# A four-layer graph kernel: largest score by transposes, earlier first attention steps, four accumulators in layer 0, eight buffers in layer 3

## What is computed

```python
# layer 0: normalised graph convolution
deg = sum(adj.T, axis=1); d = deg ** -0.5
x = x + (d[:, None] * adj.T * d[None, :]) @ (h @ W0) + b0
# layer 1: rows of adj, with 1/sqrt(count) added where adj > 0
inc = adj + (adj > 0) / max(sqrt(sum(adj > 0)), 1e-12)
x = x + (inc @ h) / sum(inc, axis=-1)
# layer 2: attention, 4 heads of 256, mean over the heads
ht = (h @ W2) per head; src = ht . a_src; dst = ht . a_dst
att = softmax(leaky_relu(src[:, None] + dst[None, :], 0.01) + adj)
x = x + mean over heads of att @ ht
# layer 3: binarised
x = x + relu(adj @ (max(sign(h), 0) @ sign(W3).T))
```

## Time and profile before

| | |
|---|---|
| median of 3 runs | 771.5 us (770.08 to 772.02) |
| profiled execution, its own time | 770.67 us |
| its span, first to last instruction | 768.8 us |
| mean granted clock of TensorE | 0.991 |
| PE busy | 729.3 us, 95% |
| DVE busy | 667.2 us, 87% |
| ACT busy | 458.7 us, 60% |
| POOL busy | 57.1 us, 7% |

### The profile page before, as it was taken

How to read it: one execution, slowest core, us unless ns; L and a number is a source line. 1 busy time by engine, 2 the same in 40 slices (tenths; PEclk the granted TensorE clock), 3 DMA queues, 4 the chain that set the end, 5 groups by cost and what they waited for, 6 DMA issues and landing times.

```text
span 768.8 us, 16799 instructions
## 1 busy us (share of the span) xinstructions
PE 729.3 (95%) x6808; PEld 619.3 (81%) x6808; DVE 667.2 (87%) x1207; ACT 458.7 (60%) x861; POOL 57.1 (7%) x87
## 2 busy tenths in 40 slices
PE   3998999989999999699999999999999999999898
PEld 3665788978888888345888888888888888888787
DVE  6887885889999997378999999999999999997583
ACT  4995100254555555476655786868686786766651
POOL 3005111101111111000000000000000000000000
PEclk9998999999999999899999999999999999999999
DMA  9986770056766642673111612026111612125592
GB/s 333 323 291 195 80 234 1 2 154 208 228 221 222 220 177 110 222 193 86 51 29 28 191 58 56 18 66 193 28 29 28 192 57 56 29 69 179 192 397 69
DMA packets 44172, 105.98 MB, mean 138 GB/s; under 512 B 3072, under 2 KB 17984, under 8 KB 39616
## 3 DMA queue, kind: packets, MB, share of 16 engines
q1 hardware_dynamic: 39824, 94.94, 36.8%
q0 software_dynamic: 4272, 9.96, 7.9%
HBM read 78.12 MB, written 18.91 MB: 126 GB/s over the span
## 4 chain that ended last, share of the span: by engine, by line
PE 72%; DVE 3%; issue 1%; ACT 1%; POOL 0%; ACTq 0%
PE ps L730 14%; PE ps L732 14%; PE ps L731 14%; PE ps L680 5%; PE ps L772 4%; PE ps L773 3%; PE ps L627 3%; PE ps L629 3%; PE ps L628 3%; PE ps L603 3%; PE ps L607 3%; PE ps L641 1%; DVE arena L1228 1%; DVE arena L1371 1%; DVE arena L1234 0%
## 5 line engine op out<-in xcount | busy, mean ns | idle before, releaser
L730 PE MATMUL ps<-arena 128*128 128x257 f16 x1024 | 279.9, 273 | 2.2 <-DVE arena L1364 2.2
L732 PE MATMUL ps<-arena 128*128 128x257 f16 x1024 | 279.4, 273 | 0.0
L731 PE MATMUL ps<-arena 128*128 128x257 f16 x1024 | 279.2, 273 | 0.0
L1037 ACT ACTIVATE arena<-arena 128x512 f16<-128x512 f32 x252 | 158.5, 629 | 95.6 <-PE ps L732 53.2
L1357 DVE SCALAR_TENSOR_TENSOR arena<-arena,w_j 128x512 f32<-128x512 f32 x256 | 189.8, 742 | 0.0
L1364 DVE TENSOR_TENSOR arena<-arena 128x512 f16<-128x512 f32 x256 | 175.4, 685 | 3.1 <-ACT arena L1037 2.6
L730 PEld LDWEIGHTS ps<-arena 128*128 128x128 f16 x1024 | 99.9, 98 | 15.4 <-issue 2.7
L731 PEld LDWEIGHTS ps<-arena 128*128 128x128 f16 x1024 | 100.3, 98 | 12.5
L732 PEld LDWEIGHTS ps<-arena 128*128 128x128 f16 x1024 | 99.8, 97 | 13.0
L869 ACT ACTIVATE arena<-ps 128x512 f16<-128x512 f32 x64 | 38.0, 593 | 56.0 <-PE ps L607 55.9
L627 PE MATMUL ps<-arena 128*128 128x257 f16 x256 | 70.3, 274 | 0.0
(11 more groups left out here) (145 smaller groups left out, 1151.2 us busy)
## 6 DMA issues: line engine op xcount, KB each, us to landing
arena<-in_adj_dram SPq DMA_DIRECT2D x32, 512.0 KB, 6.1
arena<-in_adj_dram SPq DMA_DIRECT2D x16, 1024.0 KB, 6.5
adj_t<-arena SPq DMA_DIRECT2D x16, 1024.0 KB, 7.7
arena<-adj_t SPq DMA_DIRECT2D x64, 256.0 KB, 4.1
arena<-adj_t SPq DMA_DIRECT2D x16, 1024.0 KB, 6.5
x<-arena POOLq DMA_DIRECT2D x15, 512.0 KB, 4.5
arena<-u_rows SPq DMA_DIRECT2D x4, 1024.0 KB, 13.7
x<-in_x_dram SPq DMA_DIRECT2D x4, 512.0 KB, 5.6
```

What stands on the lines that cost most here:

```text
L730: mm(ps[:, bank, 0:DE], hi, ht_hi[:, head, j, 0:DE], start=s, stop=False)
L731: mm(ps[:, bank, 0:DE], hi, ht_lo[:, head, j, 0:DE], start=False, stop=False)
L732: ins = mm(ps[:, bank, 0:DE], lo, ht_hi[:, head, j, 0:DE], start=False, stop=e)
L1037: nc.scalar.activation(p_hi[:, j % 4, :], prob[:, j % 4, :], copy).then_inc(p_hi_done, 1)
```

## The change

Six parts, on all engines:

- Layer 0 has four accumulators (`ACC0`); PE waits for the block four back. `count` and `fill` of rows 0 and 1 come at blocks 3 to 6 instead of 8 to 11, all four `w2_a` quarters at blocks 8 to 11, `w2_a_parts` at block 12.
- In layer 1 `w2_lo` is made in four quarters, after `h2_low` in rows 1 to 4. `h2_transposes` come after group 1, `scores` after group 3, and ACT's `h2_turned` after group 2.
- The largest score goes by two transposes on PE with a reduction and a spread on DVE between them, instead of POOL. The halves of `ht_block(2)` lie around the first transpose; `ht_block(3)` and `ht_high(1)` come ahead of the turn of `up_i`.
- Numerators, conversions and low parts of steps 0 to 3 come behind ht blocks 10 to 12 instead of around blocks 14 and 15. 8 instead of 10 `exp_adj` come ahead of attention.
- `at3` has eight buffers (it now also takes the place of `u_bc`). ACT waits for output block i-8 instead of i-4. DVE does `at3_low(i)` ahead of `layer3_out(i-4)`.
- In the tail of attention PE's products, turns and binary products are interleaved in a new order.

```diff
         sd = sb("sd", [P, NB, 2 * HEADS], F32)
-        dmax = sb("dmax", [P, 3, HEADS], F32)
+        dmax = sb("dmax", [P, HEADS], F32)
...
         RING3 = U + 32 * KB
-        at3 = view(RING3, [4, 2, NB, P], F16)
+        at3 = view(U, [8, 2, NB, P], F16)
...
         up_t = view(RING3 + 32 * KB, [P], F32)
+        dmax_rows = view(RING3 + 33 * KB, [P], F32)
+        dmax_top = view(RING3 + 34 * KB, [1], F32)
...
         EARLY = 4
-        E_EARLY = 10
+        E_EARLY = 8
         ACC = (0, 2)
+        ACC0 = (0, 2, 6, 7)
...
                     nc.gpsimd.partition_all_reduce(amax[:, 1:2], amax[:, 0:1], P, RMAX).then_inc(amax_all, 1)
-                if t == HBK:
+                if t == 3:
                     inverse_count(0)
-                if t == HBK + 2:
+                if t == 5:
...
-            pool.wait_ge(dmax_part, 1)
-            nc.gpsimd.partition_all_reduce(dmax[:, 1, :], dmax[:, 0, :], P, RMAX).then_inc(dmax_all, 1)
...
             def layer0(t):
-                pe.wait_ge(y_taken, t - 1)
-                bank = ACC[t % 2]
+                if t >= 4:
+                    pe.wait_ge(y_taken, t - 3)
+                bank = ACC0[t % 4]
...
                     if t < 2:
-                        pe.wait_ge(y_taken, NB - 1 + t)
+                        pe.wait_ge(y_taken, NB - 3 + t)
...
                     products1(t, g)
-                    if g == 0 and t >= 2:
+                    if g == 1 and t >= 2:
                         h2_transposes(t - 2)
-                    if g == 2 and t >= 2:
+                    if g == 3 and t >= 2:
...
-            def ht_block(t):
-                for half in range(2):
+            def ht_block(t, halves=(0, 1)):
+                for half in halves:
...
-            pe.wait_ge(w2_lo_done, 1)
+            pe.wait_ge(w2_lo_done, 4)
...
             pe.wait_ge(adjt_copied, 4 * NB)
-            ht_block(2)
...
+            ht_block(2, (0,))
...
+            pe.wait_ge(dmax_part, 1)
+            nc.tensor.transpose(ps[0:HEADS, 7, 256:256 + P], dmax[:, :], ident[:, :]).then_inc(dmax_t_ps, 1)
+            ht_block(2, (1,))
+            pe.wait_ge(dmax_spread, 1)
+            nc.tensor.transpose(ps[:, 7, 384:384 + HEADS], dmax_rows[0:HEADS, :], ident[0:HEADS, 0:HEADS]
+                                ).then_inc(dmax_all, 1)
+            ht_block(3)
...
                                 ident[:, :]).then_inc(ut_ps, 1)
-            for t in range(3, NB):
+            for t in range(4, NB):
...
             def layer3_products(i, blocks):
-                k = i % 4
+                k, bank = (4 + i) % 8, 4 + i % 4
                 for j in blocks:
-                    mm(ps[:, 4 + k, 0:D], at3[:, k, 0, j, :], xw[:, j, :], start=(j == 0), stop=False)
-                    ins = mm(ps[:, 4 + k, 0:D], at3[:, k, 1, j, :], xw[:, j, :], start=False, stop=(j == NB - 1))
+                    mm(ps[:, bank, 0:D], at3[:, k, 0, j, :], xw[:, j, :], start=(j == 0), stop=False)
+                    ins = mm(ps[:, bank, 0:D], at3[:, k, 1, j, :], xw[:, j, :], start=False, stop=(j == NB - 1))
...
             pe.wait_ge(head_scaled, (NQ * HEADS - 1) * QB)
-            for i in range(4):
-                pe.wait_ge(at3_lo_done, i + 1)
-                layer3_products(i, range(NB - QB))
+            pe.wait_ge(at3_lo_done, 2)
+            layer3_products(0, range(NB - QB))
+            layer3_products(1, range(NB - QB))
             pe.wait_ge(head_scaled, NQ * HEADS * QB)
-            for pair in range(2):
-                binary_turn(NQ - 1, pair, pair, ba_tail)
-            for pair in range(2):
-                binary_product(NQ - 1, pair, 2 + pair, bat_tail)
+            binary_turn(NQ - 1, 0, 0, ba_tail)
+            pe.wait_ge(at3_lo_done, 3)
+            layer3_products(2, range(NB - QB))
+            binary_turn(NQ - 1, 1, 1, ba_tail)
+            binary_product(NQ - 1, 0, 2, bat_tail)
+            pe.wait_ge(at3_lo_done, 4)
+            layer3_products(3, range(NB - 2 * QB))
+            binary_product(NQ - 1, 1, 3, bat_tail)
+            layer3_products(3, range(NB - 2 * QB, NB - QB))
...
                         nc.scalar.activation(w2_hi, w2_f, copy, scale=W_SCALE).then_inc(w2_hi_done, 1)
-                    if g == 1 and t >= 2:
+                    if g == 2 and t >= 2:
...
             ht_high(0)
+            ht_high(1)
...
             nc.scalar.activation(up_t[0:HEADS * NB, :], ps[0:HEADS * NB, 6, 0:P], copy).then_inc(ut_done, 1)
-            for t in range(1, NB - 2):
...
+            def first_high(j):
+                act.wait_ge(p_done, j + 1)
+                nc.scalar.activation(p_hi[:, j, :], prob[:, j, :], copy).then_inc(p_hi_done, 1)
...
+            for t in range(2, NB):
...
-            for pair in range(2):
-                for j in (2 * pair, 2 * pair + 1):
-                    act.wait_ge(p_done, j + 1)
-                    nc.scalar.activation(p_hi[:, j, :], prob[:, j, :], copy).then_inc(p_hi_done, 1)
-                ht_high(NB - 2 + pair)
+                if t in (11, 12):
+                    first_high(2 * (t - 11))
+                    first_high(2 * (t - 11) + 1)
...
                         act.wait_ge(xw_done, 2 * (NQ - 1))
-                    if i >= 4:
-                        act.wait_ge(o_ps, i - 3)
+                    if i >= 8:
+                        act.wait_ge(o_ps, i - 7)
...
                         scale_head(group - 1, 1 - b, j - 4 - late)
-                    if first and j + 6 < NB:
-                        exp_adj(0, j + 6)
+                    if first and j + 4 < NB:
+                        exp_adj(0, j + 4)
...
                     binary_input(part, NQ - 1, r, ba_tail)
-            for pair in range(2):
-                binary_turned(NQ - 1, pair, bat_tail)
+                if r == 2:
+                    binary_turned(NQ - 1, 0, bat_tail)
+            binary_turned(NQ - 1, 1, bat_tail)
...
                 dve.wait_ge(y_ps, t + 1)
-                v.scalar_tensor_tensor(x[:, t, :], ps[:, ACC[b], 0:D], dinv_out[:, t:t + 1], x[:, t, :],
+                v.scalar_tensor_tensor(x[:, t, :], ps[:, ACC0[t % 4], 0:D], dinv_out[:, t:t + 1], x[:, t, :],
...
                                     ).then_inc(amax_neg, 1)
-                if t in (HBK, HBK + 2):
-                    count((t - HBK) // 2)
-                if t in (HBK + 1, HBK + 3):
-                    fill((t - HBK) // 2)
+                if t in (3, 5):
+                    count((t - 3) // 2)
+                if t in (4, 6):
+                    fill((t - 4) // 2)
...
                     inc_low(0, t - NB + 4)
-                if NB - 4 <= t < NB - 1:
-                    if t == NB - 4:
+                if HBK <= t < HBK + 4:
+                    if t == HBK:
                         dve.wait_ge(w2_in, 32)
-                        dve.wait_ge(y_ps, 9)
-                    k = t - NB + 4
+                    k = t - HBK
                     w2_a(k // 2, (2 * (k % 2), 2 * (k % 2) + 1))
+                if t == NB - 4:
+                    w2_a_parts()
...
                     inc_low(t + 1, 0)
-                if t == 0:
-                    w2_a(1, (2, 3))
-                    w2_a_parts()
...
                     h2_low(t - 1)
-                if t == 0:
-                    dve.wait_ge(w2_hi_done, 1)
-                    v.scalar_tensor_tensor(w2_lo, w2_f, W_SCALE, w2_hi, ALU.mult, ALU.subtract
+                if 1 <= t <= 4:
+                    if t == 1:
+                        dve.wait_ge(w2_hi_done, 1)
+                    c, half = (t - 1) // 2, (t - 1) % 2 * 512
+                    v.scalar_tensor_tensor(w2_lo[:, c, half:half + 512], w2_f[:, c, half:half + 512], W_SCALE,
+                                           w2_hi[:, c, half:half + 512], ALU.mult, ALU.subtract
...
                                  1.0 / (H_SCALE * W_SCALE), None, ALU.mult))
-            v.tensor_reduce(dmax[:, 0, :], sd[:, :, HEADS:2 * HEADS].rearrange("p t h -> p h t"), AX_X, ALU.max
+            v.tensor_reduce(dmax[:, :], sd[:, :, HEADS:2 * HEADS].rearrange("p t h -> p h t"), AX_X, ALU.max
                             ).then_inc(dmax_part, 1)
+            dve.wait_ge(dmax_t_ps, 1)
+            link(v.tensor_reduce(dmax_top[0:HEADS, :], ps[0:HEADS, 7, 256:256 + P], AX_X, ALU.max))
+            v.tensor_copy(dmax_rows[0:HEADS, :], dmax_top[0:HEADS, :].broadcast_to([HEADS, P])).then_inc(dmax_spread, 1)
             dve.wait_ge(dmax_all, 1)
-            dmax_bc = dmax[:, 1:2, :].broadcast_to([P, NB, HEADS])
+            dmax_bc = ps[:, 7:8, 384:384 + HEADS].broadcast_to([P, NB, HEADS])
...
-            for t in range(NB - 2):
+            for t in range(NB):
...
-            dve.wait_ge(u_in[0], 16)
-            for pair in range(2):
-                for j in (2 * pair, 2 * pair + 1):
-                    numerators(0, 0, j, j)
-                for j in (2 * pair, 2 * pair + 1):
-                    low_part(j, j)
-                ht_low(NB - 2 + pair)
+                if t == 10:
```

(23 more changed lines are left out.)

## The result

The changed kernel takes 760.92 us (median, 758.96 to 762.12), the kernel before, run beside it, 771.76 us: ratio 0.9876, 95% interval 0.9852 to 0.9901, or 10.8 us less. The forecast was 759.9 in a range of 757.4 to 764.0. The profiled execution of the changed kernel took 762.12 us, the longest of its four; its span is 760.1.

A forecast was written before the change was run, and what follows sets the result against it. PE, at 95% of the span, bounds the kernel, so only its waits and clock losses can be won. Terms -3.1 - 3.0 - 1.7 - 2.5 + 1.1 - 2.4 = -11.6 give 759.9 us as median, range 757.4 to 764.0.

The forecast's parts named there:

- Layer 0, -2.5: Layer 0: with four accumulators and early count and fill, PE's 2.5 us of stalls go, with 2.3 us to spare.
- Layers 0 and 1, -3.1: Layer 0, seam and layer 1 together: 3.1 us less; bounds -4.4 and 0.
- The largest score, -3.0: Between last scores and ht_block(3): transposes replacing POOL's all-reduce start ht_block(3) at 322.3 instead of 325.26; bounds 2.3 and 3.2.
- Next late is ACT: Largest score: ACT's four exp_adj, 317.21 to 319.77, hold up the exps, which end at about 320.45 instead of 323.4.
- 3.2 with none of ACT's wait: Upper bound of the largest-score gain: 3.2 us if nothing waits for ACT's exp_adj.
- The clock, -1.7: ht after the largest score: PE's idle gap shrinks from 6.5 to 3.0 us, clock stays up, 1.7 us come back.
- the clock falls in the remaining gap: Rival, ht: the clock still drops in the 3 us gap, so the 1.7 is not gained; 761.6 us, 24%.
- clock 0.50 in ht: Sign of a wrong forecast: the profile would show PE's granted clock at 0.50 in ht; 1.00 was expected.
- First attention steps, -2.5 and +1.1: Attention start and ht: early steps remove 2.5 us of PE waits; extra DVE work stalls the last ht blocks by 1.1.
- Layer 3, -2.4: Start of layer 3: with eight buffers and a new tail order PE starts block 4 2.4 us sooner.
- the buffers do nothing: Rival, layer 3: despite eight buffers PE starts block 4 when it did; 762.3 us, 6%.
- u_in[0], the slower case: Rival, ht: a late u transfer makes DVE wait before numerators(0); 0.3% slower, 773.8 us, from a 31.4 us landing; 5%.

The follow-up runs named there:

- w2lo_late: Changed kernel with the four w2_lo quarters in rows 14 and 15 of layer 1 instead of rows 1 to 4; 758.45 us.
- two_acc: Changed kernel with two accumulators in layer 0 instead of four, all else of the change left; 769.8 us.
- the four above: The changed kernel, four_buf, w2lo_late and out_first, all with its ht and 2.8 us gap; they lost 1.69, 1.69, 1.56 and 1.50 us to the clock.
- steps_late: Changed kernel with numerators, conversions and low parts of attention steps 0 to 3 back around ht blocks 14 and 15; 762.81 us.
- four_buf: Changed kernel with ACT in layer 3 waiting for PE's use of the buffer four blocks back, as with four buffers; 762.9 us.
- out_first: Changed kernel with layer3_out(i-4) ahead of at3_low(i) again, eight buffers kept; 759.83 us.

## Why the prediction was right, and where it was not

Each item has the forecast in bold and the measured time difference in us behind it.

- **Layer 0, -2.5:** -2.2 in this pair, -2.3 between the means. The chain behind POOL came out to half a microsecond, and the spare was 3.3 instead of 2.3. (The prediction cites L1325's 2.28 from the earlier trace rows; it stands in the earlier trace rows.)
- **Layers 0 and 1, -3.1:** -3.25. VectorE's first late row of layer 1 (L1297, now L1317) comes 4.9 us earlier after the start of layer 0 (108.9 instead of 113.7), forecast 5.2. Each quarter of w2_lo shows as 0.5 in its row (10.0 against 9.49), 2.1 in all, for 0.6 and 2.4.
- **The largest score, -3.0:** -3.26 in this pair of profiles, -2.7 over all. The step "Next late is ACT" did not hold in the changed kernel: exp_adj began at 314.60, without its wait for the DMA, and was finished in time. The stretch so lies at the bound "3.2 with none of ACT's wait". It depends on when adj_t lands: with waits up to 0.76 (w2lo_late) the stretch stayed 5.99, and in two_acc, with 1.54, the step did hold and cost 0.5. By the Trainium skill, GPSIMD Engine Reference, section 4.1, a reduction over the partitions belongs on GpSimd; for this one, four columns of maxima, the runs show the opposite, 5.99 us against 7.5 to 10.0. Its section 2.1 gives about 6 us for freshly loaded code; here the waits were 3.8 to 6.3.
- **The clock, -1.7:** nothing in this pair, about -0.5 over all profiles. This is the step that failed: "The gaps at L603 and L772 lie beside full matmuls too and are the nearer rows, so I take -1.7". The gap of 2.8 us was enough in all five unfilled kernels that have it (the four above and steps_late). The rival "the clock falls in the remaining gap" happened; it had 24% and 761.6 us. Between known gaps of 1.8 (kept) and 6.5 (lost) the rows decided nothing, and the choice should have been nearer to even. The row at L517 was misread as well: the clock falls there in every profile, in w2lo_late at 61.2 us after no wait of PE longer than 0.5 us, so no gap of 1.7 is needed for it. And the sign of being wrong "clock 0.50 in ht" is the one that showed; the other four did not.
- **First attention steps, -2.5 and +1.1:** -2.5 and +0.74. The price was summed in part from whole durations; by pitches alone the prediction had 0.7.
- **Layer 3, -2.4:** -2.5, through the buffers (1.3) and, by subtraction, the order (1.1). That the buffers do nothing is ruled out by four_buf.
- **u_in[0], the slower case:** the longest landing was 15.3 us, and VectorE did not wait.

With 0 for the clock and 0.74 for the price the prediction's own sum is -10.3, and 761.2 us; the measured 760.9 is that within the scatter, and nearer to the rival's 761.6 than to the forecast. That 759.9 is only 1.0 off is partly luck: the one error of 1.7 was partly made up by errors of 0.1 to 0.4 the other way.

What stays open: why POOL's all-reduce takes from 3.8 to 6.3 us from its semaphore on, in one and the same program; no view shows what POOL does in that time. Open too: what decides whether the clock falls before or after TensorE begins again, and what a gap between 1.8 and 2.2 us does.

## What to carry to other kernels

A gap on TensorE costs its length and, if it is long enough, a stretch of half clock behind it: here gaps of 2.2 and 2.8 us cost 1.5 to 1.7 us more, and a dozen matmuls that nobody reads, put where the engine would wait anyway, won it back behind the gap of 2.8. A price read from one profile is one draw where it holds a wait for GpSimd (3.8 to 6.3 us in one program) or a stretch of low clock (1.7 to 2.5 in one program): profile again before a term rests on it. Where one engine times a loop row after row, put extra work on it into the rows in which its own work runs out.

## What the runs showed of the hardware that I had not expected

- The same gap of 2.8 us cost the clock at different moments. In the changed kernel and four_buf it fell 0.8 to 0.9 us after TensorE had begun again (gap 317.9 to 320.75, clock 1.00 until past 321, then 0.50 until 325); in out_first, w2lo_late and steps_late it fell 0.2 to 0.3 us before. With the gaps of 3.1 us and more it fell in the gap. In four_buf's gap of 2.2 us in layer 3 it fell 0.8 us after.
- GpSimd's all-reduce of 128 x 4 values kept VectorE waiting 3.83, 3.85, 5.01, 5.38, 5.52 and 6.30 us in six profiles; the operation itself took 0.38 or 0.39 each time. From the first all-reduce to the pow behind it POOL's row shows 7.78 us of issue in the changed kernel, 7.42 before.
